# A Swin block on one core: the MLP's narrow output half divided by token blocks and placed behind P times V, its result turned by six transposes, and another pass order in the first layer

## The reference

```python
xn = layernorm(x, ln1_w, ln1_b)
xs = roll(xn, (-3, -3)); xw = windows(xs)               # (1024, 49, 192)
q, k, v = heads(xw @ qkv_w + qkv_b)
attn = softmax(einsum('bhqd,bhkd->bhqk', q, k) * scale)
o = einsum('bhqk,bhkd->bhqd', attn, v) @ proj_w + proj_b
x = x + roll(unwindow(o), (3, 3))
h = gelu(layernorm(x, ln2_w, ln2_b) @ mlp_w1 + mlp_b1)  # 192 -> 768
x = x + (h @ mlp_w2 + mlp_b2)                           # 768 -> 192
```

## Time and profile before

| | us |
|---|---|
| median of three runs | 3240.66 |
| lowest and highest | 3238.58, 3244.01 |
| the profiled execution's own time | 3234.78 |
| span of that execution, first to last instruction | 3233.0 |

### The profile page before, as it was taken

The page is one execution under the profiler, slowest core; times in us unless marked ns, Lnnn a source line. Parts: engine busy times, 40 slices in busy tenths (PEclk is TensorE's granted clock), DMA queues, the critical chain, the costliest instruction groups (busy, mean ns, idle before and its releaser), DMA issues.

```text
span 3233.0 us, 110732 instructions
## 1 busy us (share of the span) xinstructions
PE 3174.8 (98%) x43444; PEld 2651.3 (82%) x43444; DVE 2227.1 (69%) x5903; ACT 2020.4 (62%) x3595; POOL 696.9 (22%) x785
## 2 busy tenths in 40 slices
PE   6999999999999999999999999999999999999998
PEld 6888888888888888888888888888888888888886
DVE  4677667666766676677667766766677667666764
ACT  3666666666666666666666666666666666666665
POOL 1222222222222222222222222222222222222221
PEclk8999999999999999999999999999999999999999
DMA  1010001000100010001000100000010001000100
GB/s 44 24 28 24 22 22 28 24 22 22 29 23 22 24 27 23 22 25 27 23 22 25 27 22 22 26 26 22 22 28 25 22 22 28 24 22 22 28 24 17
DMA packets 112096, 79.78 MB, mean 25 GB/s; under 512 B 10079, under 2 KB 111553, under 8 KB 112065
## 3 DMA queue, kind: packets, MB, share of 16 engines
q1 hardware_dynamic: 112064, 79.35, 9.3%
HBM read 40.78 MB, written 38.54 MB: 25 GB/s over the span
## 4 chain that ended last, share of the span: by engine, by line
PE 95%; ACT 3%; issue 1%; POOL 0%; DVE 0%; DMA 0%; SPq 0%; POOLq 0%; DVEq 0%; ACTq 0%
PE ps L743 31%; PE ps L810 16%; PE ps L746 15%; PE ps L818 8%; PE ps L778 5%; PE ps L841 5%; PE ps L861 4%; ACT vt L618 3%; PE ps L706 3%; PE ps L827 2%; PE ps L714 2%; PE ps L826 2%; PE ps L716 1%; DMA xin<-in_x 0%; POOL xb L362 0%
## 5 line engine op out<-in xcount | busy, mean ns | idle before, releaser
L743 PE MATMUL ps<-zh,w 128*128 128x392 f32 x3072 | 666.8, 345 | 22.1 <-ACT vt L618 21.4
L743 PEld LDWEIGHTS ps<-zh,w 128*128 128x128 f32 x3072 | 535.9, 188 | 63.2 <-ACT vt L618 62.4
L810 PE MATMUL ps<-g,w 128*128 128x392 f32 x1536 | 562.4, 502 | 0.0
L630 ACT ACTIVATE yT<-ps,b 128x392 f32<-128x392 f32 x256 | 150.5, 588 | 468.5 <-PE ps L818 424.4
L810 PEld LDWEIGHTS ps<-g,w 128*128 128x128 f32 x1536 | 271.4, 190 | 151.3
L743 PE MATMUL ps<-zh,wqkv 128*128 128x400 f32 x1536 | 391.7, 363 | 0.0
L666 ACT ACTIVATE g<-ps,biasf 128x392 f32<-128x392 f32 x768 | 386.2, 567 | 3.0 <-PE ps L743 1.1
L743 PEld LDWEIGHTS ps<-zh,wqkv 128*128 128x128 f32 x1536 | 281.2, 190 | 79.6 <-issue 77.0
L370 POOL TENSOR_TENSOR ve<-mv,eps 98x4 f32<-98x4 f32 x256 | 51.0, 199 | 1340.7 <-DVE mv L404 1340.7
L253 POOL TENSOR_TENSOR prob<-prob,rcp 128x588 f32<-128x588 f32 x128 | 152.2, 1189 | 867.7 <-DVE rcp L523 867.7
L412 DVE TENSOR_SCALAR z<-x,mv,rs 98x192 f32<-98x192 f32 (+2 forms) x768 | 208.6, 343 | 186.5 <-POOL rs L372 186.5
(11 more groups left out here) (94 smaller groups left out, 6021.0 us busy)
## 6 DMA issues: line engine op xcount, KB each, us to landing
xin<-in_x SPq DMA_DIRECT2D x128, 147.0 KB
out<-yo SPq DMA_DIRECT2D x128, 147.0 KB
xin<-in_x SPq DMA_DIRECT2D x128, 71.2 KB
out<-yo SPq DMA_DIRECT2D x128, 71.2 KB
xin<-in_x SPq DMA_DIRECT2D x128, 54.8 KB
out<-yo SPq DMA_DIRECT2D x128, 54.8 KB
xin<-in_x SPq DMA_DIRECT2D x128, 18.8 KB
out<-yo SPq DMA_DIRECT2D x128, 18.8 KB
```

The source lines that it names most:

```text
L743: last = pe.matmul(dst, cols(w, part), act_ if zh is zh2 else windows(act_, WIDE, EVEN), start=(n == 0), stop=(n == 4))
L810: last = pe.matmul(ps[:, Y[0], 0:M], w2[:, k, 0:A], g[:, k, :], start=(k == 0), stop=(k == KC - 1))
```

## The change

- The narrow half (`mlp2_narrow`) divides the tokens, not the chunks: for each k it makes two matmuls of 196 columns, blocks 0 and 2 into partitions 0 to 63 and blocks 1 and 3 into partitions 64 to 127. The halves are finished sums of different tokens, 12 matmuls of 196 columns in place of 6 of 392. Its bank is 6, not 3, which is also the bank of `qk`'s first tile.
- ScalarE copies it as 128 by 196 values (`narrow_result`) and the wide half as before (`wide_result`); the narrow one now comes first.
- `turn_result` is four transposes of the wide part (all in bank 2) and two of the narrow part (bank 3); `twice` and its four matmuls are gone. VectorE's `result` adds by features, 98 by 512 and then 98 by 256 values, not 98 by 384 twice.
- On TensorE the narrow half stands directly behind `pv`. The wide chunks are spread as 0 to 2 before `pv`, 3 behind the narrow half, 4 and 5 behind `proj`.
- `qk`'s first tile waits for `yT_ready` of the narrow part; the narrow half waits for all six chunks of g.
- In `mlp1` the first four chunks take the passes (0, 1, 2) chunk by chunk, then (3, 4).

In the set-up, GpSimd's making of `twice` is gone and the bias is loaded twice by a DMA.

```diff
-        twice = sb("twice", [128, B])
...
-        yT = sb("yT", [128, 2, M])
+        yT = sb("yT", [128, M])
+        yTb = sb("yTb", [128, M // 2])
...
-        Y = (7, 3)
+        Y = (7, 6)
...
-            small(b2[0:B, 1:2], mlp_b2, A, [[1, B], [1, 1]], consts_loaded)
+            small(b2[:, 1:2], mlp_b2, A, [[0, 2], [1, B], [1, 1]], consts_loaded)
...
+            def result(prev, parity):
+
+                wait(dve, stored[parity], 16 * MOVES, prev // 2, 0)
+                for part, features in enumerate((slice(0, A), slice(A, C))):
+                    n = features.stop - features.start
+                    wait(dve, ty_done, 2, prev, part + 1)
+                    dve.tensor_tensor(yo[:, parity, :, features],
+                                      ps[0:PART, TY[part], 0:BLOCKS * n].rearrange("p (q n) -> p q n", n=n),
+                                      x2[:, parity, :, features], ALU.add).then_inc(yo_done, 1)
...
-            def feature_result(prev, part):
-
-                wait(act, y_done, 2, prev, part + 1)
+            def narrow_result(prev):
+
+                wait(act, y_done, 2, prev, 1)
                 wait(act, ty_done, 2, prev - 1, 2)
-                act.activation(yT[:, part, :], ps[:, Y[part], 0:M], ACT.Identity, bias=b2[:, part:part + 1])\
-                   .then_inc(yT_ready, 1)
+                act.activation(yTb[:, :], ps[:, Y[1], 0:M // 2], ACT.Identity, bias=b2[:, 1:2]).then_inc(yT_ready, 1)
+
+            def wide_result(prev):
+
+                wait(act, y_done, 2, prev, 2)
+                act.activation(yT[:, :], ps[:, Y[0], 0:M], ACT.Identity, bias=b2[:, 0:1]).then_inc(yT_ready, 1)
...
+                if tiles == (2,):
+                    wait(pe, yT_ready, 2, i - 2, 1)
...
-                    chunk(m, (0, 1))
-                for m in first:
-                    chunk(m, (2,), {2: [(zl2_done, 2, prev, 1)]})
+                    chunk(m, (0, 1, 2), {2: [(zl2_done, 2, prev, 1)]})
...
+                wait(pe, g_done, KC, prev, KC)
                 for k in range(KC):
-                    half = slice(64 * (k % 2), 64 * (k % 2) + 64)
-                    last = pe.matmul(ps[half, Y[1], 0:M], w2[:, k, A:C], g[:, k, :], start=(k < 2), stop=(k >= KC - 2))
+                    for odd in range(2):
+                        last = pe.matmul(ps[64 * odd:64 * odd + 64, Y[1], 0:M // 2], w2[:, k, A:C],
+                                         blocks_of(g[:, k, :], odd), start=(k == 0), stop=(k == KC - 1))
                 last.then_inc(y_done, 1)
...
-                    bank, c0 = TY[p // 2], 256 * (p % 2)
-                    pe.transpose(ps[0:PART, bank, c0:c0 + A], yT[:, 0, span(p)], ident[:, :])
-                    last = pe.matmul(ps[0:PART, bank, c0 + A:c0 + C], yT[:, 1, span(p)], twice[:, :], start=True,
-                                     stop=True)
-                    if p % 2:
-                        last.then_inc(ty_done, 1)
+                    last = pe.transpose(ps[0:PART, TY[0], A * p:A * p + A], yT[:, span(p)], ident[:, :])
+                last.then_inc(ty_done, 1)
...
-                    mlp2_wide(prev, range(0, 2))
+                    mlp2_wide(prev, range(0, 3))
                 if attends(i):
                     pv(i)
                 if feeds(i):
-                    mlp2_wide(prev, range(2, KC))
+                    mlp2_narrow(prev)
+                    mlp2_wide(prev, range(3, 4))
                 if attends(i):
                     proj(i)
                 if feeds(i):
-                    mlp2_narrow(prev)
+                    mlp2_wide(prev, range(4, KC))
                 if more(i):
                     qk(i + 1, (2,))
                     qk(i + 1, (1, 0))
...
+                for h in range(BLOCKS // 2):
+                    last = pe.transpose(ps[0:PART, TY[1], 2 * B * h:2 * B * h + 2 * B], yTb[:, span(h)], ident[:, :])
+                last.then_inc(ty_done, 1)
```

More of the change, by code:

```diff
@@ L125, in swin_kernel @@
         ident_ready = sem("ident_ready")
-        twice_ready = sem("twice_ready")
         w_hi = sem("w_hi")
@@ L339, in _ @@
             pool.memset(ident[:, :], 0.0).then_inc(ident_ready, 1)
-            pool.memset(twice[:, :], 0.0).then_inc(twice_ready, 1)
             pool.wait_ge(ident_ready, 1)
@@ L343, in _ @@
                                pattern=[[-1, 128]], channel_multiplier=1).then_inc(ident_ready, 1)
-            for n in range(2):
-                pool.wait_ge(twice_ready, n + 1)
-                pool.affine_select(out=twice[:, :], in_=twice[:, :], compare_op=ALU.not_equal, fill=1.0, base=-B * n,
-                                   pattern=[[-1, B]], channel_multiplier=1).then_inc(twice_ready, 1)
             for t in (zh1[:, 0, :], zh1[:, 1, :], zl1[:, :]):
@@ L562, in body @@
                     for half in range(2):
-                        wait(dve, proj_done, 2, i, half + 1)
-                        residual(half, PROJ[half], xb[:, parity, :, :], x2[:, parity, :, :], x2_done)
+                        residual(i, parity, half)
                     wait(dve, x2_done, 2, i, 2)
@@ L573, in body @@
                 if feeds(i):
-                    result(prev, 1 - parity, 0)
-                    result(prev, 1 - parity, 1)
+                    result(prev, 1 - parity)
             iterations(dve, body)
```

20 lines of the change are left out of this document (7 added, 13 removed).

## The result

| | before | after |
|---|---|---|
| median us of four executions each | 3240.61 | 3154.82 |
| lowest and highest | 3238.58, 3244.01 | 3154.41, 3155.46 |
| ratio to before (95% interval) | | 0.9734 (0.9718 to 0.9751) |
| the profiled execution's own time | 3234.78 | 3154.41 |
| its span | 3233.0 | 3152.6 |

85.8 us less, 0.68 a body over 127 bodies; the forecast was 3149, in a range of 3118 to 3188. The page of after, by engine: busy us, share of the span, instructions; then the queue that brings instructions (packets, MB, share of time), and the shares of the chain of waits.

The account below looks back on a forecast made before the run. TensorE (PE), busy 993 of 1000 us, was taken to bound the kernel. Terms -0.27 - 0.19 + 0.02 - 0.27 = -0.71 us a body, x 127 = -90, perhaps -1 more: 3144 profiled, 3149 median, range 3118 to 3188.

Parts of the forecast that it names:

- Part 1: Pass order in mlp1: six passes ahead of the values' wait gain 0.36 us, a later wait costs 0.09; -0.27 a body.
- The stall: mlp1, fifth pass: 0.36 us a body lost at the wait for v_ready, which the new pass order removes.
- the restart: mlp1, after the wait for v_ready: 0.10 us lost because the weight load cannot run ahead; left in place.
- pass 3's wait: mlp1, pass 3 of chunk 0: VectorE's input comes late and costs 0.08 to 0.10 us, taken as 0.09.
- Part 2: Tile-shape switches on TensorE: three surcharges totalling 0.54 us become two, 0.15 and 0.20; -0.19 us a body.
- Part 3: Narrow half: twelve pairs of half length take 1.98 us as before; +0.02 us a body (0 to 0.30).
- Rival 1: Narrow half: weight loads or a fixed cost per instruction set its pace, +0.28 a body, total 3186; chance 0.10.
- Rival 4: Narrow half: instruction pairing is lost, +1.98 us a body, total 3400, slower; chance 0.04.
- Part 4: turn_result: six transposes and the switch take 0.78 us, not 1.10; waiting for q takes back 0.05; -0.27 a body.
- VectorE's lateness: Score maxima begin 0.6 us later; 0.49 vanish in the wait before zl2, 0.12 remain for mlp1's pass 3.
- Rival 2: VectorE's full 0.6 us lateness makes TensorE wait at mlp1's pass 3: +0.48 a body, total 3212; chance 0.07.
- Rival 3: No restart cost, no wait at pass 3, no wait for q: -0.95 a body, total 3120; chance 0.08.

Follow-up runs that it names:

- experiment 1: The kernel before with only the first layer's new pass order (0, 1, 2 chunk by chunk): 3197.65 us, ratio 0.9868.
- experiment 4: The changed kernel with the old pass order put back in the first layer: 3198.06 us, one execution.
- experiment 3: The changed kernel without the move, the narrow half back between proj and qk in bank 3: 3171.68 us, ratio 0.9789.
- experiment 5: The kernel before with all six narrow chunks summed in partitions 0 to 63, not alternating column halves: 3488.49 us, one execution.
- Experiment 8: The changed kernel with TensorE's wait for x2 taken off the scores and put ahead of qk's last two tiles: 3148.24 us, ratio 0.9718.
- experiment 6: The changed kernel with an unneeded VectorE memset of 600 columns behind the result's additions: 3188.42 us, one execution.
- Experiment 9: Experiment 8's kernel with ScalarE copying the values bank by bank, chunk 2 waiting for the first copy, chunk 3 for the second: 3143.69 us, ratio 0.9704.

## Why the prediction was right, and where not

**Part 1** (-0.27; measured -0.33, shown by experiments 1 and 4). The stall and the restart came as worked out: the seventh pass on pace, then 0.08 to 0.09 lost where 0.10 were allowed. The term that was mis-sized is pass 3's wait: 0.09 were set for it and none came, because VectorE was not late (below). Without it the part would have read -0.36; the last 0.03 are not traced to one term.

**Part 2** (-0.19; measured -0.13, experiment 3). That surcharges stand at tile-shape switches, and that one of the three goes, was right, as were the two that stay: 0.15 for pv to narrow, chosen between 0.15 and 0.19, and 0.19 for narrow to full where 0.20 was set. The term that was mis-sized is qk: it has no surcharge at its head, as forecast, but its passes take 0.193 us where the prediction read 0.19 from before. That reading was right for before (0.190); that the pace would change was not foreseen, and fifteen passes make 0.04 of it. The wide chunks before qk took 0.02 more.

**Part 3** (+0.02; measured +0.01). Twelve pairs go at 0.166 us each, half of the 0.33 of a long pair. Rival 1, the weight loads or a fixed cost as pace, fell: 24 instructions take what 12 took. The fixed cost of some 60 cycles a matmul, which the prediction weighed by the Trainium skill's TensorEngine Tiling (Array Packing), section Instruction Overhead, doesn't show at 196 columns: by it 0.30 us would have been added, and 0.01 was. Rival 4 fell with it, and experiment 5 shows by what condition the pairing holds; its price was 1.98 in the prediction, and 1.96 was measured in the narrow group.

**Part 4** (-0.27; measured -0.27 in one body, -0.16 in the next). In the better body the turn took the 0.83 us that were worked out, 0.78 and 0.05 of waiting for q; how it splits can't be read, since no kernel here with six transposes starts the scores without that wait. From the end of q's copy to the scores are 0.05 us where 0.04 was set. The step that failed is that a wait costs only its semaphore: q's wait stands on an instruction of its own ahead of the first load in every second body, and there the scores start 0.14 us behind the copy. The period of these bodies is 0.11 longer. Experiment 8 takes the separate instruction away, and the loop's bodies become 3.9 us shorter together.

**VectorE's lateness** was overstated. The maxima were to start at 1.6 us and started at 1.2. z2 ended 0.33 after the scores' start where 0.51 were worked out, because TensorE's part between proj and the scores shrank by 1.1 us in this body and not by 1.28. And 1.06 us for the result's two additions were added behind it although they begin 0.09 before it ends (1605.75 + 1.63 = 1607.38, against 1607.29), and the maxima 0.09 before the additions end. Neighbours on VectorE that wait for nothing overlap so in the trace of before too: zl2 (L428) ends at 1603.16 there and the maxima behind it start at 1603.07. So the wait before zl2 shrank from 0.49 to about 0.25 a body and did not vanish, and pass 3 did not wait. The chain itself is sound: experiment 6 pushed it by 0.65 and got 0.265 in the period. Rival 2 (3212) would have needed that.

**The sum.** Part 1 brought 0.06 more than forecast, Part 2 0.06 less and Part 4 0.055 less (mean of two bodies): -0.67 a body and not -0.71. The first two errors cancel. That the forecast of 3149 stood only 5.8 us below the result is in part luck of another kind. Traced against traced, 3144 was forecast and 3154.41 came, 10.4 us more. Half of that is the bodies of the loop; the other half is the first and last bodies, for which -0.71 each and a further -1 were counted and which together brought 0.3 us, with the clock at 0.5 in after's last one. Then 5.9 us were added because the median of before stood so far above its profiled execution; the median of after stands 0.4 above its own. This second error hid half of the first.

Rival 3 (3120) counted on no wait for q, no restart and one more surcharge gone. Experiment 9 brings only the second, at 3143.69, and found the next wait 0.1 us behind; q's copy still ends the wait of the scores' first load in all its bodies.

## What to carry to other kernels

A wait in the middle of a "busy" TensorE is found by the spacing of matmul starts, and an order of passes that puts the independent ones in front of it gives its whole length back, whatever else is changed; look then for what is late next and for how far it is, here 0.1 us. Small matmuls that fill half of the array's columns cost nothing extra if neighbours in the program alternate between the halves, and shorter, more numerous ones are as good as long ones at 196 columns; group them so that the program goes from one tile shape to another as seldom as it can. An instruction on the critical path should carry one wait only: put those that are long fulfilled somewhere earlier. Changing the order of two waits in the source is not enough, and after such an edit the trace has to be asked where each wait went. And compare a traced execution with a traced one, and medians with medians: here the two differences are 80.4 and 85.8 us.

## What the runs showed of the hardware that was not expected

**A second wait costs time when the one in front is met late.** With q's wait on an instruction of its own ahead of the load the scores start 0.14 us after q's copy, with it on the load 0.05. Before has the same separate instruction in the same 61 bodies and pays nothing: q came 0.31 us early there.

**A longer loop body can lose what loops give.** Two bodies a turn: 22 packets and 0.36 MB of instructions in the whole run. Four: 410 packets and 6.72 MB, TensorE idle for 0.96 and 1.78 us at places inside the bodies, its granted clock at 0.5 for some microseconds behind them, and 171 us more. After's TensorE runs 44,212 matmul instructions and as many weight loads in 129 bodies, some 685 a body; with the sequencer's own the trace has 713 in a body of the loop, 1426 in a turn of two and some 2850 in a turn of four; between these two the code stopped being kept, as I read it; no run tried a size between. The Trainium skill, Runtime: NRT & Kernel Launch, section Instruction fetch mechanics, gives TensorE room for 2048 instructions, refilled in blocks of 16 KiB, and says that a taken branch whose target isn't among the pages held forces a fetch before execution goes on. The trace agrees with the blocks, 6.72 MB in 410 packets being 16 KiB each, and it doesn't speak against the 2048, which lies between 1426 and 2850. The stops, however, stand in pv and in the scores, not only at the loop's branch.

**Surcharges at tile-shape switches** are 0.15 to 0.20 us each, into narrow and out of it alike.

**The pace of the same passes differs between builds.** qk's fp32r passes of 400 columns take 0.190 us in before and in experiment 3 and 0.193 in after and in experiment 1, at a granted clock of 1.00; why is open.
